# Retention's third outer product of each batch moved a chunk later, its key turns moved ahead, and the join to the next stage reordered

## The chip, the cores and the metric

The kernel runs on one core of one Trainium2 chip. The metric is device time in microseconds (us), the median of several executions. One further execution is recorded by the hardware profiler; its span is the time from the first to the last instruction.

## The reference, cut to what matters

The program is a two-layer decoder on x of shape (2, 512, 256). Layer 0 is a Performer attention, a self and cross attention, and a routed expert block. Layer 1 is a retention, two blocks of softmax attention (a1 on x itself, a2 on a memory), and a routed SwiGLU block. The change touches retention and the first steps of a1:

```python
x = x + L1_attn(layernorm(x), W_qkv, W_o, log_gamma)     # retention, 16 heads of 16
    q, k, v = split((x @ W_qkv.T).reshape(B, L, 3, H, dk))
    k = layernorm(k)
    gamma = sigmoid(log_gamma)
    step: S = gamma * S + v_t[:, None] * k_t[None, :];   y_t = S @ q_t
    y @ W_o.T
x = x + L1_xattn(layernorm(x), ...)                      # first of it: a1
    x = ln(xx, ln1_g, ln1_b)
    a1: xn = ln(x, lnx_g, lnx_b);  yn = ln(x, lny_g, lny_b)
        q = xn @ wq;  k = yn @ wk;  v = yn @ wv;  a = softmax(q k^T / sqrt(32)) ...
```

## The kernel before

Tokens lie in 8 chunks of 128 (4 to a batch, SC = 4; NC = 8), features in FC = 2 blocks of 128. Each engine (TensorE, VectorE, ScalarE, GpSimd as POOL, SyncE) runs its own program; all of them walk the same hand-written list of steps and meet by semaphores. PSUM has 8 banks of 128 x 512 f32, handed out by rings (`Banks.open`): a step that opens a bank waits until its last user has been read out.

Retention is computed in chunks. For chunk c of batch b:
- "scores" (`tensor_scores`, L3632): keys by queries within the chunk, 16 small products into banks 0 to 3, as 32 instructions. VectorE then multiplies them with the decay table (`vector_decay`, L3824, two instructions of 1024 elements), which frees the banks for the next chunk's scores.
- "outer" (`tensor_outer`, L3617): weighted keys by values of chunk i, for i = 0, 1, 2 of each batch. It opens a bank of `ring` (banks 6 and 7). VectorE masks it (`vector_state`, L3806) and adds the decayed earlier state (L3814). The state after chunk i is read by the values of chunk i + 1.
- "key_turn" (`tensor_key_turn`, L3608): the normalised keys (`vector_key_norm`, L3790) turned by TensorE, copied by ScalarE (L3720). Those of batch 1 use `ring` as well, and are needed from the scores of chunk 4 on.
- "values" (`tensor_values`, L3647 for the state's part, L3650 for the chunk's own) into `value_banks` (4 and 5), copied by ScalarE (L3723).
- "rows" (`tensor_rows`, L3661): the output projection of the chunk into `ring`. VectorE adds it to x (L445) and takes the statistics (L281). After chunks 3 and 7 the norm of four chunks follows: a root on ScalarE, scales on VectorE, the application on ScalarE, VectorE and POOL.

The list of steps in the middle, for c from 0 to 9, is: scores c; at c = 0 the three outer products of batch 0; at c = 1 the key turns of batch 1; at c = 2 the three outer products of batch 1; values c - 1; at c = 9 "turn_ahead"; rows c - 2.

"turn_ahead" is the first half of a1's turn: `Turn.tensor` (L382) turns the normalised rows of chunks 0 to 3, one bank of `ring` for each feature block, with six filling matmuls (L175) into the first bank ahead of it. `Turn.scalar_copies` (L398) makes two forms from each bank: `xnT`, for the queries, and `a1ynT`, for keys and values, in the order xnT, ynT of block 0, then xnT, ynT of block 1. VectorE's part of a1's norm for these chunks is done after the rows of chunks 5 and 6 (`ahead`). Then a1's `lead_in` begins: key and query projections (`HeadProjection`, L1810) by turns, and from the fourth projection on the maxima of scores (L1570 on TensorE, L1729 on VectorE) among them. A key projection waits for `ready_x`, which is the last copy of each bank; that same mark frees the bank.

Of the kernel before, what the change touches and what calls it, by code (L numbers as in the profile page):

```python
# [351 lines left out]
class Turn:  # L352
# [35 lines left out]
    def scalar_copies(self, e, w, n):  # L388
        for f in range(self.width // P):
            if not self.by_scalar(f, n):  # L390
                continue
            w.wait_ge(*self.turned.at(self.name, f, n))
            if self.affine is None:
                e.activation(self.dst[:, f, cols(n)], self.view(f, n), ACT.Copy).then_inc(*self.scalar.mark(self.name, f, n))
                continue
            for i, (dst, gain, shift) in enumerate(self.affine):
                w.wait_ge(*self.k.columns.ready.at())
                e.activation(dst[:, f, cols(n)], self.view(f, n), ACT.Identity, bias=shift[:, f:f + 1], scale=gain[:, f:f + 1]).then_inc(  # L398
                    *self.scalar.mark(self.name, f, n, i) if i < len(self.affine) - 1 else self.scalar.mark(self.name, f, n))

# [2553 lines left out]
class Mha:  # L2954
# [4 lines left out]
    def __init__(self, k, pre, before, ready, cross, gain=None, shift=None, norm=None):  # L2959
# [13 lines left out]
        with ExitStack() as mem:  # L2973
# [15 lines left out]
            with ExitStack() as att:  # L2989
# [13 lines left out]
                with ExitStack() as tmp:  # L3003
# [12 lines left out]
                    if not cross:  # L3016
                        self.keys = HeadProjection(
                            k, pre + "_pk", self.attention, self.w["wk"], self.loads["wk"], FC, lambda f, n: self.ynT[:, f, cols(n)], ready_x, self.kT, self.kr)
                for b in range(B):
# [340 lines left out]
class Retention:  # L3360
# [90 lines left out]

    def order(self):

# [7 lines left out]
        for c in range(NC + 2):  # L3461
            if c < NC:
                yield "scores", c
            if c == 0:
                yield from (("outer", (0, i)) for i in range(SC - 1))
            if c == 1:
                yield from (("key_turn", (m, 1)) for m in range(FC))
            if c == 2:
                yield from (("outer", (1, i)) for i in range(SC - 1))
            if 0 <= c - 1 < NC:  # L3470
                yield "values", c - 1
            if c == NC + 1:
                yield "turn_ahead", 0
            if c >= 2:
                yield "rows", c - 2


# [66 lines left out]
    def tensor_program(self, e, w):  # L3544
        opened = False
        for step, i in self.order():
            if step == "scores" and not opened:
# [55 lines left out]
    def tensor_key_turn(self, e, w, m, b):  # L3603
        k = self.k
        bank = (self.ring if b else k.banks).open(w, ("re_kT", m, b), self.k_copied.at(m, b))
        w.wait_ge(*self.knormed.at(b))
# [642 lines left out]
```

## Time and profile before

| | |
|---|---|
| median of 3 runs | 1537.38 us |
| lowest and highest | 1536.84 and 1538.34 us |
| the profiled execution's own time | 1538.35 us |
| its span | 1536.6 us |
| mean granted TensorE clock | 0.987 |
| TensorE busy | 95% of the span |
| scores of chunk 0 begin | 735.23 us |
| a1's first key projection begins | 781.94 us |

Times in views count from the start of the span. The profiled execution's own time lies 1.75 us above its span and 0.97 us above the median of the others. TensorE is PE, its weight loads are PEld. A matmul in f32 appears as two records, a transpose as one. In a timeline, consecutive instructions of one line are merged: the start of the first, the time to the end of the last, and how many. In a window, the numbers are its length, the busy time and count of PE, PEld, DVE, ACT and POOL, then the granted clock, the DMA engines' share and GB/s.

### The profile page before, as it was taken

How to read it: one execution, taken by the hardware profiler on the slowest of the kernel's cores; microseconds unless marked ns; L12 is line 12 of the kernel's file. 1: busy time of each engine (PE TensorE's matmuls, PEld its weight loads, DVE VectorE, ACT ScalarE, POOL GpSimd, SP SyncE). 2: the span in 40 equal slices, each digit the busy share in tenths (PEclk: the TensorE clock that was granted, in tenths of full speed). 3: DMA queues.
4: the chain of work that ended last, by engine and by line, in shares of the span. 5: the costliest groups of instructions: out<-in, count | busy, mean ns of one | idle time of the engine just before them, and what ended most of it. 6: DMA issues, size and time to landing. Idle time of an engine off the chain costs nothing.

```text
span 1536.6 us, 24700 instructions
## 1 busy us (share of the span) xinstructions
PE 1456.1 (95%) x9894; PEld 818.6 (53%) x9894; DVE 851.8 (55%) x1816; ACT 720.3 (47%) x1079; POOL 586.3 (38%) x653
## 2 busy tenths in 40 slices
PE   8999999999999988899899999998999999997997
PEld 5678873333333256796643333653333333766997
DVE  3256627668999564136753784348777772323221
ACT  4544324675666645233254456433555556332331
POOL 3043306223424333521022565502777777405111
PEclk9999999999999999899999999999999999998999
DMA  6000000000110048673000001403000000653000
GB/s 218 1 1 1 1 11 1 8 8 15 49 36 21 3 145 291 206 237 43 7 21 1 1 1 56 124 0 130 1 1 1 1 1 29 242 190 126 9 12 9
DMA packets 75208, 86.94 MB, mean 57 GB/s; under 512 B 27161, under 2 KB 60917, under 8 KB 73942
## 3 DMA queue, kind: packets, MB, share of 16 engines
q1 hardware_dynamic: 72182, 79.10, 16.3%
q0 software_dynamic: 2912, 6.26, 1.1%
q8 instruction: 78, 1.28, 0.3%
q14 instruction: 36, 0.29, 0.1%
HBM read 64.25 MB, written 21.37 MB: 56 GB/s over the span
## 4 chain that ended last, share of the span: by engine, by line
PE 83%; DVE 9%; ACT 3%; issue 2%; POOL 1%; another core or an unknown queue 1%; DMA 0%; POOLq 0%; DVEq 0%; ACTq 0%
PE psum L1606 13%; PE psum L1625 9%; PE psum L1570 7%; PE psum L3997 5%; PE psum L717 4%; PE psum L3263 4%; PE psum L3254 4%; DVE a_nm L1729 3%; PE psum L1810 3%; PE psum L1647 3%; PE psum L4008 2%; PE psum L2740 2%; PE psum L757 2%; PE psum L3232 2%; PE psum L705 2%
## 5 line engine op out<-in xcount | busy, mean ns | idle before, releaser
L1729 DVE TENSOR_REDUCE a_nm<-psum 128x1 f32<-128x512 f32 x384 | 248.9, 685 | 99.5 <-PE psum L1570 87.9
L1729 DVE TENSOR_REDUCE xa_nm<-psum 128x1 f32<-128x512 f32 x256 | 161.7, 682 | 49.5 <-PE psum L1570 44.2
L1660 ACT ACTIVATE a_w<-psum 128x1024 f32<-128x1024 f32 x86 | 83.3, 1021 | 60.7 <-PE psum L1606 60.7
L1660 ACT ACTIVATE xn<-psum 128x1024 f32<-128x1024 f32 (+1 forms) x96 | 86.2, 949 | 51.5 <-PE psum L1606 51.5
L1606 PE MATMUL psum<-a2qT,a2kT 32*128 32x512 f32 x512 | 90.2, 592 | 0.0
L1660 ACT ACTIVATE xa_w<-psum 128x1024 f32<-128x1024 f32 (+2 forms) x96 | 79.7, 886 | 19.2 <-PE psum L1606 19.1
L1570 PE MATMUL psum<-a2kr,a2qr 32*128 32x512 bf16 x256 | 78.1, 384 | 7.4 <-DVE a_nm L1729 5.5
L1570 PEld LDWEIGHTS psum<-a2kr,a2qr 32*128 32x128 bf16 x256 | 20.5, 91 | 108.5 <-DVE a_nm L1729 92.5
L1570 PE MATMUL psum<-xa_ckr,xa_cqr 32*128 32x512 bf16 x256 | 65.7, 382 | 1.7 <-POOL xa_ckr L1857 1.0
L1602 PE MATMUL psum<-a_mrow,onesb 3*128 3x512 bf16 x384 | 62.4, 386 | 3.6 <-DVE a_mrow L1752 1.5
L4064 DVE TENSOR_TENSOR sw_hT<-sw_gt,psum 128x512 f32<-128x512 f32 x22 | 15.0, 688 | 71.3 <-PE psum L3997 43.6
L651 POOL TENSOR_SCALAR pf_kdd<-pf_kdd 128x1024 f32<-128x1024 f32 x8 | 22.2, 2773 | 84.2 <-ACT pf_kdd L830 84.1
L3936 POOL DMA_INDIRECT out<-sw_o,sw_back x11 | 15.2, 1381 | 101.4 <-DVE sw_o L4082 84.2
L1726 DVE TENSOR_REDUCE xa_parts<-psum 128x4 f32<-128x512 f32 x80 | 50.1, 677 | 6.7 <-PE psum L1568 4.4
L1606 PE MATMUL psum<-xa_cq,ctxT 32*128 32x512 f32 x256 | 53.3, 636 | 0.1
L1570 PEld LDWEIGHTS psum<-xa_ckr,xa_cqr 32*128 32x128 bf16 x256 | 17.3, 91 | 65.3 <-DVE xa_nm L1729 47.9
L1660 ACT ACTIVATE ctxT<-psum 128x1024 f32<-128x1024 f32 x40 | 38.8, 1021 | 25.7 <-PE psum L1606 25.0
L1660 ACT ACTIVATE xnT<-psum 128x1024 f32<-128x1024 f32 x40 | 38.8, 1021 | 24.1 <-PE psum L1606 24.1
L1570 PE MATMUL psum<-a1kr,a1qr 32*128 32x512 bf16 x128 | 42.5, 383 | 5.0 <-DVE a_nm L1729 4.0
L1606 PE MATMUL psum<-xa_cq,co_ctx 32*128 32x512 f32 x256 | 46.6, 629 | 0.0
L3997 PE MATMUL psum<-sw_xgT,sw_own 128*128 128x128 f32 x384 | 44.1, 275 | 0.5 <-ACT sw_xgT L4046 0.5
L1606 PE MATMUL psum<-a1qT,a1kT 32*128 32x512 f32 x256 | 44.5, 587 | 0.0
(582 smaller groups left out, 3404.5 us busy)
## 6 DMA issues: line engine op xcount, KB each, us to landing
mo_w<-in_L_ffn_W SPq DMA_DIRECT2D x14, 1024.0 KB
sw_wv<-in_L_ffn_w_v SPq DMA_DIRECT2D x4, 2048.0 KB, 18.7
scratch_a2v<-co_stages SPq DMA_DIRECT2D x16, 256.0 KB
scratch_a2k<-co_stages SPq DMA_DIRECT2D x16, 256.0 KB
a2kT<-scratch_a2k SPq DMA_DIRECT2D x8, 512.0 KB, 8.6
a2v<-scratch_a2v SPq DMA_DIRECT2D x4, 1024.0 KB, 11.6
sw_wp<-in_L_ffn_w_proj SPq DMA_DIRECT2D x4, 1024.0 KB, 19.6
scratch_yd<-zero SPq DMA_DIRECT2D x8, 256.0 KB, 2.2
```

What stands on the lines that cost most here:

```text
L717: t = e.matmul(k.ps[:, bank, :], wt[:, f, chunk(pair)], k.xnT[:, f, cols(n)], start=f == 0, stop=f == FC - 1)
L1570: t = e.matmul(out, query[:, chunk(i)], key[:, part * S:(part + 1) * S], start=True, stop=True)
L1602: e.matmul(ps[:, pr + h % 2, lo:S], self.k.const.onesb[rows, :], self.mrow[n % 3][rows, lo:S], start=True, stop=False)
L1606: t = e.matmul(ps[:, pr + h % 2, lo:S], job.key(h)[:, chunk(c)], job.query(h)[:, lo:S], start=self.folded, stop=True)
L1625: t = e.matmul(ps[32 * h:32 * h + 32, 6, lo:hi], job.value(c, h), self.weights(n, c)[:, h, lo:hi], start=start, stop=last and not upper)
L1647: t = e.matmul(ps[32 * h:32 * h + 32, 7, :], self.k.const.ones[:, 0:32], self.weights(n, c)[:, h, :], start=(n, c) == self.dens(n)[0], sto ...
L1660: e.activation(self.weights(n, c)[:, 2 * jj:2 * jj + 2, lo:S], ps[:, pr:pr + 2, lo:S], ACT.Exp, scale=self.scale).then_inc(*self.weighed.m ...
L1726: e.tensor_reduce(self.parts[n % 3][:, q, part, :], view.rearrange("p (h n) -> p h n", n=P), AX.X, ALU.max, negate=True).then_inc(*self.ma ...
L1729: e.tensor_reduce(self.nm[n % 3][:, q, part, h:h + 1], view, AX.X, ALU.max, negate=True).then_inc(*self.max_taken.mark(*i))
L3254: t = e.matmul(k.ps[:, bank, :], self.li2[:, f, chunk(m)], k.xnT[:, f, cols(n)], start=f == 0, stop=f == FC - 1)
L3263: t = e.matmul(self.k.ps[:, self.k.banks.of(self.rows.name, c), 0:D], self.hT[:, m, chunk(c)], self.li3[:, m, :], start=m == 0, stop=m == ...
L3997: t = e.matmul(k.ps[:, bank, chunk(j)], self.own[i % 2][f][:, features], self.xgT[i % 2][:, chunk(f)], start=f == 0, stop=f == FC - 1)
```

## The change

The list of steps gets a form for TensorE alone, and four things move. The third outer product of each batch comes one chunk later on all engines (at c = 1 and c = 3). The key turns of batch 1 come at c = 0, behind the first two outer products, and use the banks of the values. On TensorE "turn_ahead" comes behind the rows of chunk 7; on the other engines the place stays. And ScalarE makes the keys' form (ynT) of both blocks first and then the queries' form; the key projections of a1 wait for the keys' form alone, while a bank is still free only after its queries' form.

```diff
+            else:
+                self.scalar_affine(e, w, f, n, len(self.affine) - 1)
+        for i in reversed(range(len(self.affine or ()) - 1)):
+            for f in range(self.width // P):
+                self.scalar_affine(e, w, f, n, i)
+
+    def scalar_affine(self, e, w, f, n, i):
+        dst, gain, shift = self.affine[i]
+        w.wait_ge(*self.k.columns.ready.at())
+        e.activation(dst[:, f, cols(n)], self.view(f, n), ACT.Identity, bias=shift[:, f:f + 1], scale=gain[:, f:f + 1]).then_inc(
+            *self.scalar.mark(self.name, f, n, i) if i else self.scalar.mark(self.name, f, n))
+
+    def form_copied(self, f, n, i):
+        return self.scalar.at(self.name, f, n, i)
...
                         self.keys = HeadProjection(
-                            k, pre + "_pk", self.attention, self.w["wk"], self.loads["wk"], FC, lambda f, n: self.ynT[:, f, cols(n)], ready_x, self.kT, self.kr)
+                            k, pre + "_pk", self.attention, self.w["wk"], self.loads["wk"], FC, lambda f, n: self.ynT[:, f, cols(n)],
+                            lambda n: [self.xturn.form_copied(f, n, 1) for f in range(FC)], self.kT, self.kr)
...
-    def order(self):
+    def order(self, tensor=False):
...
             if c < NC:
                 yield "scores", c
+            if c in (0, 2):
+                yield from (("outer", (c // 2, i)) for i in range(2))
             if c == 0:
-                yield from (("outer", (0, i)) for i in range(SC - 1))
-            if c == 1:
                 yield from (("key_turn", (m, 1)) for m in range(FC))
-            if c == 2:
-                yield from (("outer", (1, i)) for i in range(SC - 1))
+            if c in (1, 3):
+                yield "outer", (c // 2, 2)
             if 0 <= c - 1 < NC:
                 yield "values", c - 1
-            if c == NC + 1:
+            if c == NC + 1 and not tensor:
                 yield "turn_ahead", 0
             if c >= 2:
                 yield "rows", c - 2
+        if tensor:
+            yield "turn_ahead", 0
...
-        for step, i in self.order():
+        for step, i in self.order(tensor=True):
...
-        bank = (self.ring if b else k.banks).open(w, ("re_kT", m, b), self.k_copied.at(m, b))
+        bank = (self.value_banks if b else k.banks).open(w, ("re_kT", m, b), self.k_copied.at(m, b))
```

## Rows read from the trace of the kernel before

**Rows 1.** The page: busy time by engine, and the chain by engine

```profile
PE 1456.1 (95%) x9894; PEld 818.6 (53%) x9894; DVE 851.8 (55%) x1816; ACT 720.3 (47%) x1079; POOL 586.3 (38%) x653
...
PE 83%; DVE 9%; ACT 3%; issue 2%; POOL 1%; another core or an unknown queue 1%; DMA 0%; POOLq 0%; DVEq 0%; ACTq 0%
```

**Rows 2.** The chain that ended last, in order of time (start, us, what)

```profile
737.02 2.35 DVE re_w L3824 x2
739.37 0.41 DVE re_state L3806 x2
```

**Rows 3.** Timeline of TensorE, retention (start us, us, engine, line)

```profile
732.90 1.04 PE L3608 MATMUL psum<-ident,re_kt 128*128 128x128 f32 x8
735.23 1.17 PE L3632 MATMUL psum<-re_q,re_kT 32*128 32x128 f32 x32 [1.29 <-ACT re_kT L3720]
736.33 1.16 PE L3617 MATMUL psum<-re_v,re_kw 128*128 128x128 f32 x8
739.82 1.03 PE L3617 MATMUL psum<-re_v,re_kw 128*128 128x128 f32 x4 [2.33 <-DVE re_state L3806]
...
754.07 0.49 PE L3647 MATMUL psum<-re_qg,re_state 128*128 128x128 f32 x2
...
756.06 1.13 PE L3661 MATMUL psum<-rew_woT,re_yT 128*128 128x256 f32 x4
757.12 1.17 PE L3632 MATMUL psum<-re_q,re_kT 32*128 32x128 f32 x32
```

**Rows 4.** Timeline of VectorE, retention

```profile
735.88 1.22 DVE L3790 TENSOR_TENSOR re_kt<-re_kt,re_kst 128x1024 f32<-128x1024 f32 x1
...
740.88 0.49 DVE L3806 TENSOR_TENSOR re_state<-psum,block 128x128 f32<-128x128 f32 x2
741.48 0.61 DVE L3814 SCALAR_TENSOR_TENSOR re_state<-re_state,rew_whole 128x128 f32<-128x128 f32 x2
742.94 2.36 DVE L3824 TENSOR_TENSOR re_w<-psum,rew_decay 128x1024 f32<-128x1024 f32 x2 [0.85 <-PE psum L3632]
```

**Rows 5.** Busy time in chosen windows; the third number from the end is the clock

```profile
739.80:743.40 3.60, 3.58 (x39) 3.13 (x40) 2.54 (x9) 0.00 (x0) 0.00 (x0) 0.54 0.00 0
...
747.70:749.40 1.70, 0.00 (x1) 0.00 (x0) 1.70 (x5) 0.00 (x0) 0.00 (x0) 1.00 0.00 0
749.40:757.10 7.70, 7.62 (x116) 5.48 (x116) 5.24 (x13) 0.77 (x2) 0.00 (x0) 1.00 0.00 0
...
777.60:780.40 2.80, 1.52 (x8) 0.87 (x8) 0.51 (x2) 2.38 (x5) 0.00 (x0) 1.00 0.00 0
780.90:784.40 3.50, 3.50 (x7) 1.63 (x6) 1.79 (x10) 1.22 (x4) 0.00 (x0) 0.52 0.00 0
...
1024.00:1026.00 2.00, 0.81 (x8) 0.60 (x7) 0.80 (x2) 1.45 (x2) 0.00 (x0) 1.00 0.00 0
1026.00:1028.00 2.00, 1.86 (x4) 0.55 (x4) 0.00 (x0) 0.10 (x1) 0.00 (x0) 1.00 0.00 0
```

**Rows 6.** Timeline of TensorE at the join to a1

```profile
776.10 1.46 PE L175 MATMUL psum<-mask_four,identb 128*128 128x512 bf16 x6
777.84 1.57 PE L382 MATMUL psum<-ident,ctxT 128*128 128x128 f32 x8 [0.28 <-DVE ctxT L313]
780.51 1.62 PE L3661 MATMUL psum<-rew_woT,re_yT 128*128 128x256 f32 x4 [1.10 <-ACT a1ynT L398]
781.94 3.19 PE L1810 MATMUL psum<-a1ynT,a1wk 128*128 128x512 f32 x4
784.97 1.88 PE L1810 MATMUL psum<-xnT,a1wq 128*128 128x512 f32 x4
```

**Rows 7.** Timeline of ScalarE at the join: first and last of four copies

```profile
779.01 0.78 ACT L398 ACTIVATE xnT<-psum,cols 128x512 f32<-128x512 f32 x1 [0.42 <-PE psum L382]
...
781.02 0.78 ACT L398 ACTIVATE a1ynT<-psum,cols 128x512 f32<-128x512 f32 x1
```

**Rows 8.** Timeline of VectorE: last of a1's second half norm

```profile
790.13 0.73 DVE L313 TENSOR_SCALAR ctxT<-xn,a_norm_agg,a_norm_std 128x256 f32<-128x256 f32 x2
```

More of the change, by code:

```diff
@@ L394, in scalar_copies @@
                 e.activation(self.dst[:, f, cols(n)], self.view(f, n), ACT.Copy).then_inc(*self.scalar.mark(self.name, f, n))
[L395 to L399, printed above, removed]
+            else:
[10 more added lines that the diff above has]
+        return self.scalar.at(self.name, f, n, i)
     def vector_copies(self, e, w, n):
```

## The prediction

> **What bounds the kernel now.** I read the page first. TensorE is busy 95% of the span and carries 83% of the chain that ended last; VectorE has 9% of it [rows 1]. So time is saved only where the chain leaves TensorE, or where TensorE runs at its lower clock. I then read the chain in order of time over retention. For the first scores it stands on VectorE: the decay product of chunk 0, then the mask of the first outer product, and only then a TensorE instruction [rows 2]. The timeline of TensorE shows the stalls: 2.33 us before the third outer product of batch 0 (739.82) [rows 3], and nothing at all on TensorE from 747.7 to 749.4, ahead of the third of batch 1 [rows 5]. The reason is in the ring of two banks: the third outer product takes the bank of the first, which VectorE masks only after a decay product that lasts 2.35 us. After the first stall the clock was granted at 0.54 over 739.8 to 743.4, and at 1.00 after the second [rows 5]. The third place is the join to a1: row block 7 waits 1.10 us on ScalarE's copies of a1's turn, whose bank it needs, and from 780.9 to 784.4 the clock is 0.52 [rows 5, 6].
>
> **The third outer product a chunk later, the key turns ahead.** Nothing is added or removed: the same matmuls, masks and copies, in another order. I place them one after another.
> TensorE: scores 0 from 735.23 to 736.33 (1.10) and two outer products (1.16 for eight records at full clock) to 737.49 [rows 3]. The two key turns of batch 1 now follow; the keys are normalised at 737.10 [rows 4], just in time, and their banks are those of the values, unused so far. They take 1.04 [rows 3], to 738.53. Scores 1 need both decay products of chunk 0, which end at 739.37 [rows 2]. With 0.14 of lag (my allowance for one wait between engines) they start at 739.51: a wait of 1.0 in place of 2.33, with the turns done.
> They end at 740.61. VectorE masks and carries two outer products, as now, to 740.88, where the third one's mask stands today [rows 4]. That mask and its carry take 1.21 (740.88 to 742.09) and move behind decay 1. So decay 1 starts at 740.9 instead of 742.94 [rows 4], ends at 743.26, and the moved pair ends at 744.4. Meanwhile TensorE does the moved outer product (0.58) and values 0, whose length is below the 1.99 of a full values step (754.07 to 756.06) [rows 3], so it is free at 743.2 at the latest.
> Scores 2 start at 743.40 and end at 744.50; outer products to 745.66 (the second one's bank is masked by 743.8); values 1 (1.99) to 747.65; row block 0 (756.06 to 757.12, 1.06) to 748.71. Decay 2 runs on VectorE from 744.5 to 746.9 and is over when scores 3 start at 748.71: the second stall is gone, covered by values 1 and row block 0. Scores 3 to 749.81, outer product to 750.39 (its bank masked by 748.4), values 2 to 752.38, row block 1 to 753.44. Scores 4 start there; now they start at 757.12 [rows 3]. That is **3.7 us**. From there the order is the old one. The copies of the key turns on ScalarE come earlier, in front of nothing; the values behind them wait for nothing new. SP and POOL are passed by no step: POOL's weighted keys are made before, and SP's next loads wait for the last rows, which come earlier.
> Bounds: the stalls cannot give more than they hold, 2.33 + 1.7 less the new 1.0 and about 0.2 at scores 2, plus the slow stretch, which holds 3.6 us at 0.54 and so hides at most about 1.8: 4.6. From below, if the clock falls again, scores 1 take some 2.2, decay 1 begins at 741.7 and all behind it 0.8 later: 2.9. I take 3.7, since it is made of rows at full clock.
>
> **The last row block ahead of a1's turn.** In times of before, so as to leave the 3.7 out. Row block 7 now needs bank 7 from row block 5 and its copied values, both there; it follows row block 6 at once, 776.2 to 777.3. The six fills (1.46 now, 1.29 back to back) end at 778.55; the turn's first bank is that of row block 6, which VectorE adds while TensorE does row block 7. The first transpose then starts at 778.55 where it starts at 777.84 now [rows 6]; but the last of the first four waits for its chunk now, until about 778.6 (ScalarE starts at 779.01, some 0.4 behind it [rows 7]), so the first bank is full only 0.3 later. The turn ends at 779.6. The second bank needs VectorE's addition of row block 7, which stands behind VectorE's share of a1's norm; the turn needs that share from 777.84 on anyway, and both should be done by 778.6, 0.4 before the bank is asked for. ScalarE copies from 779.3 instead of 779.01 [rows 7].
>
> **The keys' form first.** Four copies of 0.67 pitch (779.01 to 781.02 is three) [rows 7]. Now the first key projection waits for all four and for row block 7, and starts at 781.94 [rows 6]. After the change it waits for two: 779.3 + 0.67 + 0.78 is 780.75, so 780.8. That is **1.15**. The query projection behind it comes at 782.5 and needs all four copies, done at 782.1: covered by the first key projection, with 0.4 to spare; without that cover it would cost up to 1.3.
> The clock is the other half. The first projection lasts 3.19 us, the next, the same four matmuls at full clock, 1.88 [rows 6]: **1.3** lost. TensorE after the change works without a gap from the rows to 779.6 and then waits 1.2. The nearest row is the same join of a2's turn: it was granted 1.00 over 1024 to 1026 with TensorE busy 0.81 of 2.00 us, eight transposes before and one wait in it, and kept it [rows 5]. I take the 1.3 as won; both ends, 0 and 1.3, stay in the range.
> The second half of a1's normalisation hangs on row block 7 and on ScalarE, which takes up the root after the four copies, at 782.1. It now ends at 790.86 on VectorE [rows 8]; if it came no earlier, the first maxima, 2.4 us earlier on TensorE, would wait behind it with two banks to run ahead in: at most about 1 us. Row block 7 is done at 782.1 now and its addition, statistics and scales come before that root; so the root at 782.1 is over 1 us earlier than today's, and I take 0.
> **Sum:** 3.7 + 1.15 + 1.3 = 6.15. The profiled execution took 1538.35, of which 1536.6 is span and 1.75 lies around it; it becomes 1532.2. Against the median of 1537.38, 0.97 lower, the forecast is **1531.2**.
>
> **A rule against it.** The granted clock fell after 777.6 to 780.4, in which TensorE was busy 1.52 of 2.80 with little but transposes, and stayed up after a stretch of 1.7 with nothing in it, at 747.7 [rows 5]. The Trainium skill (TensorE: Matmul & The Clock Gate, Part 4: PE-mode transpose) says that a transpose does not count as busy work for the clock in the way that a matmul does. By that rule the key turns are poor cover at 737.5 and the a1 turn keeps its slow stretch. The rows at 777.6 agree with it, and those at 1024 do not show it. By rule and row together the sum would be 2.9 + 1.15, that is 1533.3; by the rows at 1024, 1531.2.
>
> **The rivals.**
> (a) The clock falls at the key turns, at a1's join, or at both. For it: a fall at each place now, with transposes in one of them. Against: the waits are 1.0 and 1.2 instead of 2.3 and two of about 1.1 around sparse transposes. Price 0.8, 1.3 or 2.1: 1532.0, 1532.5, 1533.3.
> (b) The gain is given back in a1's lead-in: VectorE's and ScalarE's second-half normalisation, or the query projection, becomes late. Price 1 to 2.5: 1532.2 to 1533.7. Against it: both have slack above, though only some tenths for the query.
> (c) The change does not remove retention's waits: the moved masks stand behind decay 1 and 3, and the next outer product finds its bank taken. It is asked for at 745.1 and masked at 743.8, so 1.3 of slack; beyond that every tenth counts. If both waits return in full, only a1's 2.45 stays: 1534.9.
> (d) Slower: the work behind, shifted by 6 us, meets the clock's falls at other stalls. One fall costs 1.3 here (first projection). It takes five to undo the sum, and more than seven for over 0.2% slower; at seven the time is 1540.3, at eight 1541.6. The span has far more waits of 1 to 2 us than falls, so it can be; nothing in the trace points to it. A single one more or less moves the forecast by 1.3 either way.
>
> **How the numbers follow.** The forecast's own case gets 0.60, with 1.3 on each side for one clock fall elsewhere: 1529.9 to 1532.5. (a) gets 0.20, (b) 0.10, (c) 0.07, (d) 0.03. About 0.2%, 3.1 us, is what a measurement of this kernel can tell from no change. The forecast, (a) and (b) lie beyond it: 0.90, less 0.02 for (a) and (b) together: faster 0.88. (c) and that 0.02 are within: 0.09. Slower 0.03. The range reaches from 1529.5 (half of what the bound of 4.6 has over 3.7, and one fall fewer) to 1533.9, which takes in (a) and (b).
>
> **What would show it.** Scores 1 start at 739.5, with the two key turns of batch 1 ahead of them; scores 2 at 743.4; no idle time on TensorE before an outer product; scores 4 at 753.4. Row block 7 directly behind row block 6, then fills, turn, and a wait of 1.2 ended by a copy of a1's ynT; the first key projection at 777.1 (780.8 less 3.7), its four matmuls in 1.7 us at a granted clock of 1.00. The forecast is wrong if the clock is near 0.5 in either place, if an outer product waits on a state, if the first query projection waits on xnT, or if a maximum early in a1 waits on VectorE for over 0.5.

## The result, and the profile after

Twenty executions of each kernel, side by side, gave medians of 1539.88 us before (1536.84 to 1558.49) and 1535.99 us after (1530.66 to 1541.18): the ratio of all executions is 0.9964, with a 95% interval of 0.9947 to 0.9980. The two medians alone give 0.9975, a difference of 3.9 us, and the two means differ by 5.2, since before has one execution at 1558.49. The three runs of before that were shown ahead of the prediction belong to these twenty and are among the faster ones. The forecast of 1531.2 is 0.9960 of their 1537.38. That is inside the interval of the ratio, though not met by the medians; as a time it lies 4.8 us too low and its range, 1529.5 to 1533.9, misses the median.

First the timeline of TensorE after, retention, as in [rows 3]. The line numbers have moved by 12: L3644 is scores, L3629 outer, L3620 key turn, L3662 and L3659 values, L3673 rows.

```profile
734.63 1.17 PE L3644 MATMUL psum<-re_q,re_kT 32*128 32x128 f32 x32 [1.28 <-ACT re_kT L3732]
735.73 1.16 PE L3629 MATMUL psum<-re_v,re_kw 128*128 128x128 f32 x8
736.72 1.04 PE L3620 MATMUL psum<-ident,re_kt 128*128 128x128 f32 x8
738.92 1.17 PE L3644 MATMUL psum<-re_q,re_kT 32*128 32x128 f32 x32 [1.15 <-DVE re_w L3836]
740.02 0.71 PE L3629 MATMUL psum<-re_v,re_kw 128*128 128x128 f32 x4
740.66 1.08 PE L3662 MATMUL psum<-re_w,re_v 128*32 128x128 f32 x32
742.69 1.17 PE L3644 MATMUL psum<-re_q,re_kT 32*128 32x128 f32 x32 [0.95 <-DVE re_w L3836]
...
747.79 1.17 PE L3644 MATMUL psum<-re_q,re_kT 32*128 32x128 f32 x32
748.89 0.71 PE L3629 MATMUL psum<-re_v,re_kw 128*128 128x128 f32 x4
...
752.39 1.17 PE L3644 MATMUL psum<-re_q,re_kT 32*128 32x128 f32 x32
```

The waits in front of an outer product are gone. What is left, 1.15 and 0.95, stands in front of scores and ends with a decay product. From scores 0 to scores 4 it is 752.39 - 734.63 = 17.76 us; before, 757.12 - 735.23 = 21.89.

The same view at the join, as in [rows 6], and ScalarE's copies as in [rows 7]:

```profile
770.40 1.99 PE L3673 MATMUL psum<-rew_woT,re_yT 128*128 128x256 f32 x8
772.23 1.46 PE L175 MATMUL psum<-mask_four,identb 128*128 128x512 bf16 x6
773.53 1.15 PE L382 MATMUL psum<-ident,ctxT 128*128 128x128 f32 x8
775.87 1.96 PE L1819 MATMUL psum<-a1ynT,a1wk 128*128 128x512 f32 x4 [1.19 <-ACT a1ynT L404]
777.66 1.88 PE L1819 MATMUL psum<-xnT,a1wq 128*128 128x512 f32 x4
...
774.28 1.45 ACT L404 ACTIVATE a1ynT<-psum,cols 128x512 f32<-128x512 f32 x2 [0.42 <-PE psum L382]
775.62 1.44 ACT L404 ACTIVATE xnT<-psum,cols 128x512 f32<-128x512 f32 x2
```

Row blocks 6 and 7 are one group, fills and turn follow, and the first key projection starts when the second copy of ynT is done. It lasts 1.96 where it lasted 3.19. From the first scores to the second projection it is 43.03 us, and was 49.74: **6.71 won**. Yet the span fell only from 1536.6 to 1533.9. The windows of after show where the rest went (the clock is the third number from the end):

```profile
734.60:739.00 4.40, 3.22 (x52) 2.92 (x53) 4.27 (x6) 1.15 (x3) 1.50 (x1) 1.00 0.02 6
739.00:743.00 4.00, 3.05 (x77) 2.57 (x81) 3.84 (x9) 0.38 (x1) 0.00 (x0) 1.00 0.00 0
...
775.80:780.00 4.20, 4.13 (x10) 2.01 (x11) 2.70 (x6) 3.75 (x8) 1.58 (x2) 1.00 0.00 0
828.00:832.70 4.70, 3.58 (x27) 1.71 (x27) 2.91 (x5) 3.39 (x4) 0.00 (x0) 1.00 0.00 0
832.70:839.60 6.90, 6.90 (x42) 2.49 (x39) 2.52 (x4) 2.48 (x3) 2.89 (x4) 0.51 0.01 2
...
1051.20:1054.60 3.40, 3.40 (x6) 0.67 (x5) 1.78 (x3) 0.00 (x0) 0.00 (x0) 0.50 1.05 391
1075.10:1078.50 3.40, 3.40 (x22) 1.15 (x22) 2.18 (x4) 0.82 (x1) 1.40 (x2) 0.50 0.00 0
```

The two slow stretches of before, in retention and at the join, are gone. Two new ones have come, in work that the change does not touch: at a1's first scores (832.7 to 839.6) and in a2's lead-in (1051.2 to 1054.6). The one near 1076 was there before as well, and so were those that lie further from the change, between 611 and 638 and near 1406. I measured the program in stretches between the same first instructions in both traces, by their starts:

| stretch | before | after | difference |
|---|---|---|---|
| start to retention's first scores | 735.23 | 734.63 | -0.60 |
| scores 0 to scores 4 | 21.89 | 17.76 | -4.13 |
| scores 4 to scores 7 | 12.08 | 12.08 | 0 |
| scores 7 to a1's first key projection | 12.74 | 11.40 | -1.34 |
| first to second projection | 3.03 | 1.79 | -1.24 |
| to a1's first scores | 52.35 | 52.35 | 0 |
| to a1's first column sums | 12.14 | 14.91 | +2.77 |
| to a2's first query projection | 176.45 | 176.51 | +0.06 |
| to a2's first scores | 47.38 | 48.99 | +1.61 |
| to the end | 463.31 | 463.48 | +0.17 |

The differences sum to -2.70, the change of the span. Nearly all that was given back, 4.38, lies in the two stretches with a new slow clock. So theory T after the result was: the change's own steps won what was forecast, and the remainder is where the clock falls elsewhere. The rival R: a fixed wait of the changed kernel's own takes it back.

### The profile page after: what moved, and what is told of

Read it like the earlier page. It is cut to its first block, busy times and chain, and to the rows that moved or that the text cites. A ratio compares the mean times of both kernels' runs of the same rounds, so it can differ in the third digit from the quotient of the medians.

```text
span 1533.9 us, 24703 instructions
## 1 busy us (share of the span) xinstructions
PE 1455.4 (95%) x9894; PEld 818.0 (53%) x9894; DVE 852.0 (56%) x1816; ACT 720.2 (47%) x1079; POOL 587.2 (38%) x653
## 4 chain that ended last, share of the span: by engine, by line
PE 84%; DVE 9%; ACT 2%; issue 2%; POOL 1%; another core or an unknown queue 1%; DMA 0%; POOLq 0%; DVEq 0%; ACTq 0%
PE psum L1615 13%; PE psum L1634 9%; PE psum L1579 7%; PE psum L4009 5%; PE psum L726 4%; PE psum L3273 4%; PE psum L3264 4%; DVE a_nm L1738 3%; PE psum L1819 3%; PE psum L1656 3%; PE psum L4020 2%; PE psum L2749 2%; PE psum L766 2%; PE psum L3242 2%; PE psum L714 2%
## 5 line engine op out<-in xcount | busy, mean ns | idle before, releaser
L660 POOL TENSOR_SCALAR pf_kdd<-pf_kdd 128x1024 f32<-128x1024 f32 x8 | 22.2, 2774 | 81.4 <-ACT pf_kdd L839 81.3
L2749 PE MATMUL psum<-mo_xgT,mo_w 128*128 128x154 f32 x256 | 37.8, 309 | 7.6 <-DVE mo_xgT L2730 7.4
```

The lines of the kernel that those rows point to most:

```text
L2749: t = e.matmul(ps[:, bank, (m - m0) * 256:(m - m0) * 256 + CAP], w1[:, f, chunk(m)], self.xgT[:, f, x * CAP:(x + 1) * CAP], start=f == 0, ...
```

## The experiments

**Both kernels again, and the two halves of the change.** before_again and after_again are the two files unchanged. ret_only takes back the join, join_only takes back retention's part. The core of each edit against the changed kernel:

```diff
-            if c == NC + 1 and not tensor:
+            if c == NC + 1:
...
-        if tensor:
-            yield "turn_ahead", 0
...
-                            lambda n: [self.xturn.form_copied(f, n, 1) for f in range(FC)], self.kT, self.kr)
+                            ready_x, self.kT, self.kr)
```

for ret_only, with the copies in the old order as well, and for join_only:

```diff
-            if c in (0, 2):
-                yield from (("outer", (c // 2, i)) for i in range(2))
             if c == 0:
+                yield from (("outer", (0, i)) for i in range(SC - 1))
+            if c == 1:
                 yield from (("key_turn", (m, 1)) for m in range(FC))
-            if c in (1, 3):
-                yield "outer", (c // 2, 2)
+            if c == 2:
+                yield from (("outer", (1, i)) for i in range(SC - 1))
...
-        bank = (self.value_banks if b else k.banks).open(w, ("re_kT", m, b), self.k_copied.at(m, b))
+        bank = (self.ring if b else k.banks).open(w, ("re_kT", m, b), self.k_copied.at(m, b))
```

> The kernel before, unchanged, as a control. Theory T (the two profiled executions of before and after agree in their work outside retention and a1's join; what differs there is where TensorE's clock fell): a second profile of the same kernel shows the same 49.7 us from the first scores to a1's second projection, give or take 1.7, but falls of the clock in other places than the first one, and a span that differs from 1536.6 by 1 to 4 us with them. Rival R (the 4 us that after gives back are a fixed wait of its own): the span comes within 0.5 us of 1536.6 and the falls stand where they stood. Ratio to before: 1.000, and the spread of its single times shows what a median of three is worth.

> The changed kernel, unchanged, as a control. T: 43.0 us from the first scores to a1's second projection, as in its first profile; falls of the clock at other places than 832 to 840 and 1051 to 1055, and where one of these is missing, the stretch around it is 1.4 to 3 us shorter than in the first profile of after. R: the stretches from a1's join to the end are again some 4 us longer than in before, wherever the clock falls. Ratio 0.996 to 0.997 for both, as it is the same kernel as the one measured.

> Retention's part alone: third outer products a chunk later and key turns ahead in the values' banks; the join to a1 as before. T: scores 4 begin 17.8 us after scores 0 (before 21.9, after 17.8), and a1's second projection 45.6 after scores 0: before's 49.7 less 4.1, as the join keeps its wait of 1.1 and its slow projection. Ratio about 0.9973. R, in the form that the join eats what retention wins: the join takes more than before's 27.85 from scores 4 to the second projection.

> The join alone: row block 7 ahead of a1's turn and the keys' form copied first; retention as before. T: scores 4 at 21.9 as in before, the second projection 25.3 after scores 4 as in after (before 27.85): 2.6 won, ratio about 0.9983. If the clock falls at the join all the same, 1.3 of it stays away. R: less than 1 us is won, because row block 7 ahead only helps when retention has ended early.

Measured on one chip, twelve executions each, medians: before 1538.08, after 1533.61, retention's part 1535.67, the join's 1540.00. Their ratios to a further 35 executions of before there are 0.9958, 0.9923, 0.9943 and 0.9972. The first of these is the kernel before against itself, and its interval (0.9922 to 0.9994) does not even hold 1: seven of the 35 took 1555 to 1559 us. So medians of a dozen cannot settle parts of 2 us here, and the traces have to.

In the traces the stretches repeat to 0.1 us where the clock is 1.00: scores 0 to 4 took 17.77 with retention's part alone and 17.76 again with all. Join_only took 23.47 where I had expected 21.9, with a slow stretch at each of the old waits, the second of them new. Scores 7 to the first projection took 11.41 with the join's part and 12.74 without. The halves add. Wrong was what I expected of where the clock falls: I had expected other places in a second profile of the same kernel, and from retention on before_again and after_again showed the same stretches slow as their first profiles (a1's first scores to the column sums 12.14 and 14.91). A third profile of each, below, did differ. But ret_only shows none of the new ones: 12.15 there, 47.39 to a2's scores, and a span of 1531.0, which is 2.9 less than the full change, although its join is 1.3 us longer. I had expected a slow first projection there, as in before; it took 1.79 to the second, so 44.4 from the first scores instead of 45.6, although the join's steps are those of before:

```profile
777.64 1.96 PE L1817 MATMUL psum<-a1ynT,a1wk 128*128 128x512 f32 x4 [0.30 <-ACT a1ynT L402]
```

So the slow first projection is no fixed cost of that join. Seven profiles in all have the join of before (before, before_again, before_third, ret_only, outer_only, outer_values and turns_only); in two of them, before and before_again, the projection is slow. R (a fixed wait of the changed kernel) does not fit that, and T (scatter by chance) does not fit the two repeats. Theory T2: a stall late in the program drops the clock or not by the moment at which it comes, so everything that shifts the work moves the falls.

**The same kernel shifted by fills.** Filling matmuls into the bank of a1's first key projection, ahead of its wait:

```diff
-        self.attention.beside.open(w, (self.name, m, n), self.kept_exact(m, n))
+        bank = self.attention.beside.open(w, (self.name, m, n), self.kept_exact(m, n))
+        if self.name == "a1_pk" and (m, n) == (0, 0):
+            self.k.fill(e, w, self.k.ps[:, bank, :], 13)      # 5, 13 or 20
```

hold instead puts fills where the clock fell: four in the wait between the first two score pairs of a1 and a2, and 3, 1, 1 ahead of maxima in a2's lead-in, each in a bank that is opened next anyway.

```diff
+        if self.own_den and (n, c, jj) == (0, self.chunks(0)[1], 0):
+            for point in self.acc_free:
+                w.wait_ge(*point)
+            self.k.fill(e, w, ps[:, 7, :], 4)
...
+                if self.cross and step == "max":
+                    since += 1
+                    if since in (3, 4, 5):
+                        self.fill_beside(e, w, 3 if since == 3 else 1)
```

> The changed kernel with five filling matmuls ahead of a1's first key projection, in the 1.19 us in which TensorE waits there for ScalarE's copies. They delay nothing (five take about 1.1). Theory T2 (which stalls the clock falls at is settled by when the later work arrives, not by this wait): first key projection within 0.2 of 775.9 counted alike from the first scores, and the same slow stretches as the changed kernel, 2.8 lost between a1's first scores and its first column sums and 1.6 before a2's scores. Theory R2 (the clock fell later because TensorE waited at the join): these two are gone, and the span is 4 us shorter, near 1529.5.

> The same with 13 filling matmuls, which delay everything behind by about 1.7 us. T2: the work of a1 arrives about where the retention-only kernel has it (there 96.7 us from the first scores to a1's first scores, 95.4 in the changed kernel), and in the profiled execution the slow stretch at a1's first scores is missing as it is there; the kernel pays 1.7 and gets back up to 2.8 + 1.6: span 1531 to 1533, below the 1533.9 of the changed one though it does more. R3 (the slow stretches belong to the order of the join's steps, whatever the time): both stay, span 1535.6.

> The same with 20, a delay of about 3.2 us. T2 cannot say from one point where the next slow stretches come; if they follow the arrival time alone, they differ from those of the 5 and 13 fills in at least one place. R3: both stay, and the span is 1537.1. Timed runs: each fill beyond five costs 0.216 in every execution, so if falls scatter by themselves, medians rise by 1.7 and 3.2 over the changed kernel, whatever the profile shows.

> The changed kernel with fills at the two places where its clock fell: four in the wait of 0.9 between the first two pairs of scores of a1 (and of a2), and three, one, one in the waits before the third to fifth maxima behind a2's second turn. T2: the slow stretches at 832 and 1051 are gone, and perhaps the one at 1075; 2.8 + 1.6 less about 0.4 for fills that don't fit their waits: span near 1530, ratio against the changed kernel 0.997 to 0.998 in the profiled execution, and a lower median and a narrower spread of the timed ones. If the spread stays as wide, the falls that make it lie elsewhere, before retention too.

| | scores 7 to first projection | a1 scores to sums | a2 projection to scores | span | median |
|---|---|---|---|---|---|
| after (first profile) | 11.40 | 14.91 | 48.99 | 1533.9 | |
| delay5 | 11.40 | 12.15 | 47.39 | 1531.4 | 1536.84 |
| delay13 | 12.85 | 12.15 | 57.36 | 1547.1 | 1539.03 |
| delay20 | 14.36 | 12.14 | 47.38 | 1535.6 | 1540.03 |
| hold (median of five) | 11.41 | 12.14 | 47.84 | 1533.3 | 1535.00 |

On that chip 28 further executions of before had a median of 1541.70.

Five fills delay nothing, and both new slow stretches are gone in the profile. T2 had said that both stay, so by itself this speaks for R2 (the join's wait causes them). But the work before the join came 1.56 us later in that execution (first scores at 736.19, not 734.63), so the moment changed too, and the run tells the two apart less well than I meant it to. Thirteen fills speak against R3 and against R2 for a2's stretch: the order of the steps is the same and the join's wait is filled, a1's stretch is fast, and a2's is 10 us longer. For a1's stretch R2 is weakened only by turns_only below, which has the join of before and is slow there all the same (13.50). The windows of delay13 from a2's turn on:

```profile
1046.00:1053.80 7.80, 6.55 (x32) 3.22 (x30) 5.98 (x14) 4.09 (x8) 4.23 (x4) 1.00 0.69 209
1053.80:1070.00 16.20, 14.63 (x25) 3.33 (x24) 7.87 (x13) 2.26 (x5) 0.00 (x0) 0.50 0.56 207
1070.00:1091.30 21.30, 18.70 (x67) 6.43 (x69) 11.31 (x19) 7.24 (x9) 8.12 (x14) 0.50 0.00 1
1091.30:1100.00 8.70, 8.58 (x72) 2.59 (x65) 6.25 (x11) 5.82 (x6) 7.34 (x6) 1.00 0.00 0
```

One slow stretch, 37.5 us long. So my figure for this run (span 1531 to 1533) was missed by 14, in the direction that T2 leaves open: it says that falls move with the shift, not that they become fewer. Twenty fills gave the same picture as five, one slow stretch at a2's first scores (1076.5 to 1079.9) between the join and 1400, so a shift does not always move a fall. The medians follow the work: 2.2 and 3.2 more than with five fills, for 8 x 0.216 = 1.7 and 15 x 0.216 = 3.2.

T2 is therefore not shown. Each shifted kernel was profiled once, so moment and chance are not parted, and the time from the start of the span does not settle it: a1's first scores began at 831.55 in delay5, which kept the clock, and at 831.96 in after_third, which lost it. What the traces show is that the same stall loses the clock in one execution and keeps it in another.

hold missed as well: a span near 1530 was expected and 1533.3 came. The slow stretches at 832 and 1051 are gone, but a2's first scores have one of 10.2 us, and the four fills there did not stop it, since it begins ahead of them:

```profile
1066.80:1077.00 10.20, 9.87 (x46) 3.39 (x46) 4.91 (x9) 3.82 (x5) 4.96 (x7) 0.50 0.01 2
```

Part of the scatter between executions lies ahead of the change, where the kernels are the same: the first scores began between 733.47 us (before_again) and 741.07 (outer_values), with the clock down for 10.2 and 20.5 us of the time before them.

**One move at a time.** outer_only moves the third outer products and leaves the key turns; turns_only does the reverse; row7_only and form_only split the join.

All four are made from the halves. outer_only, against ret_only:

```diff
-            if c == 0:
+            if c in (1, 3):
+                yield "outer", (c // 2, 2)
+            if c == 1:
                 yield from (("key_turn", (m, 1)) for m in range(FC))
-            if c in (1, 3):
-                yield "outer", (c // 2, 2)
...
-        bank = (self.value_banks if b else k.banks).open(w, ("re_kT", m, b), self.k_copied.at(m, b))
+        bank = (self.ring if b else k.banks).open(w, ("re_kT", m, b), self.k_copied.at(m, b))
```

turns_only, against ret_only:

```diff
-            if c in (1, 3):
+            if c in (0, 2):
                 yield "outer", (c // 2, 2)
```

row7_only, against join_only, with the copies in the old order as well:

```diff
-                            lambda n: [self.xturn.form_copied(f, n, 1) for f in range(FC)], self.kT, self.kr)
+                            ready_x, self.kT, self.kr)
```

form_only, against join_only:

```diff
-            if c == NC + 1 and not tensor:
+            if c == NC + 1:
...
-        if tensor:
-            yield "turn_ahead", 0
```

> Of the four moves only the third outer products, a chunk later; batch 1's key turns stay at c = 1, in the ring's banks; the join as before. By the steps of the prediction the decay product of chunk 0 still ends at the same time and lets scores 1 begin, and TensorE reaches scores 2 with all its work done before decay 1 ends: 17.8 us from scores 0 to scores 4, as with all moves. TensorE then waits 2.0 in one piece ahead of scores 1. If the clock falls in it (rival: the key turns are what keeps it up) it is 18.6.

> Only the key turns ahead, in the values' banks, behind two outer products; the third outer product behind them still at c = 0 and c = 2. The first wait shrinks from 2.3 to 1.2, the second stays (1.8). 20.9 us from scores 0 to scores 4 (21.9 before) if the clock holds at the first wait; rival (the turns count for nothing and the clock falls as before): 21.9 less about 0.3.

> Only row block 7 ahead of a1's turn; copies in the old order, and the key projection waits for all four. From the start of scores 7 to the first key projection: the turn is full 0.3 later and four copies follow, so 12.9 (before 12.74, with both moves 11.40): nothing won. TensorE waits 2.5 there, so the clock most likely falls and the first projection lasts 3.0 as before. Rival (the row block was the bound): 11.4 to 11.7.

> Only the keys' form first; row block 7 still behind the turn, in the bank of the turn's first block, which is free after the queries' form, now the third copy instead of the second: it begins 0.65 later, and the key projection behind it at 13.0 after scores 7 (before 12.74): lost 0.3. Rival (the copies were the bound): 11.6.

This chip is quicker by 22 us for the kernel before too (1515.57 in one execution beside 1510.78, 1513.81, 1518.09 and 1514.30 of these four), so only stretches are compared. turns_only took 20.85 from scores 0 to 4, as expected (20.9): the first wait 1.46 instead of 2.33, the second as before. row7_only took 12.74 from scores 7 to the first projection and form_only 12.94, expected 12.9 and 13.0: each alone wins nothing, together 1.34 (before 12.74, both 11.40). With row block 7 ahead, ScalarE's four copies are the bound; with the keys' form first, row block 7 is, since it waits for xnT. row7_only also has the slow first projection, 3.37.

Three of these kernels also tell what the clock alone was worth in retention, which the first two profiles could not. form_only and row7_only have the steps of before there, with the slow stretch in another place; turns_only has none.

| us from scores to scores | 0 to 2 | 2 to 3 | 3 to 4 |
|---|---|---|---|
| before, slow from 740.1 to 743.5 | 10.21 | 7.53 | 4.15 |
| form_only, slow from 734.9 to 738.3 | 9.17 | 9.02 | 4.15 |
| row7_only, slow from 728.2 to 731.6 | 9.92 | 7.54 | 4.15 |
| turns_only, not slow | 9.17 | 7.53 | 4.15 |

The steps of before at one clock take 9.17 + 7.53 + 4.15 = 20.85, an estimate from these rows. So of the 4.13 won in retention 3.09 is the new order and 1.04 is the slow stretch of before. turns_only takes the same 20.85: the key turns ahead win no time by themselves.

outer_only was the miss: 21.14 where I expected 17.8 (before 21.89). Its timeline of TensorE:

```profile
721.52 1.17 PE L3640 MATMUL psum<-re_q,re_kT 32*128 32x128 f32 x32 [1.29 <-ACT re_kT L3728]
722.62 1.16 PE L3625 MATMUL psum<-re_v,re_kw 128*128 128x128 f32 x8
725.81 1.17 PE L3640 MATMUL psum<-re_q,re_kT 32*128 32x128 f32 x32 [2.03 <-DVE re_w L3832]
726.91 0.71 PE L3625 MATMUL psum<-re_v,re_kw 128*128 128x128 f32 x4
727.46 0.60 PE L3616 MATMUL psum<-ident,re_kt 128*128 128x128 f32 x4
729.88 0.66 PE L3616 MATMUL psum<-ident,re_kt 128*128 128x128 f32 x4 [1.82 <-DVE re_state L3814]
730.47 1.20 PE L3658 MATMUL psum<-re_w,re_v 128*32 128x128 f32 x32
731.59 2.09 PE L3640 MATMUL psum<-re_q,re_kT 32*128 32x128 f32 x32
```

The second key turn waits 1.82 us for a state's mask: in the ring of two its bank is that of the outer product just moved, whose mask stands behind decay 1. It is rival (c)'s mechanism, in a step that the change had moved out of its way.

**Side by side once more, the bank alone, and more fills.** before_third and after_third are the unchanged files. outer_values is outer_only with the key turns in the values' banks. Its edit against outer_only:

```diff
-        bank = (self.ring if b else k.banks).open(w, ("re_kT", m, b), self.k_copied.at(m, b))
+        bank = (self.value_banks if b else k.banks).open(w, ("re_kT", m, b), self.k_copied.at(m, b))
```

hold2 is hold with a fill ahead of the third maximum in a row, and of each further one in that row, from a2's first stretch of maxima behind its second turn on:

```diff
-                    if since in (3, 4, 5):
-                        self.fill_beside(e, w, 3 if since == 3 else 1)
+                    if 3 <= since < 99:
+                        self.fill_beside(e, w, 3 if turned and since == 3 else 1)
...
+            elif step in ("feature", "query", "row"):
+                turned, since = False, 0 if self.cross and since < 99 else 99
```

> The kernel before once more, beside the changed one and on the same chip as it. Its timed executions scatter by several us, with a lower mean clock in the longer ones. Theory T2: the ratio of this kernel to itself is 1.000 within its interval, and medians of changed and unchanged kernel on one chip differ by what the profiles show as fixed, 5.5 us (4.1 in retention and 1.3 at the join, clock aside), give or take the falls of the clock: 4 to 7.

> The changed kernel beside it. T2: 17.76 us from scores 0 to scores 4 and 11.40 from scores 7 to the first key projection, as each time; median 4 to 7 us under the other's, ratio 0.9955 to 0.9975. Rival R (the shift gives the gain back by itself): a difference under 3.

> The changed kernel with fills in the waits of a1's first scores, and in those of a2's lead-in and first scores wherever TensorE waits there for VectorE (third of three maxima in a row, and the tail). T2: no slow stretch between 825 and 1080 in the profiled execution, none of the executions over 1545, and a median 1 to 3 us under the changed kernel's. Rival: the fills cost what they save, because VectorE's maxima are the bound there; then the stretch from a2's first query projections to its first scores is longer than 47.4 at a clock of 1.00.

> The third outer products a chunk later, the key turns of batch 1 at c = 1 as in before, but in the values' banks. It tells whether the move of the outer products alone won little (21.1 us from scores 0 to scores 4 instead of the 17.8 expected) because of the bank or because of the place. If the bank: 17.8 to 18.7, and no wait of a key turn on a state's mask. If the place: 21.1 again.

| twelve executions (hold2 eleven) | median | lowest | highest |
|---|---|---|---|
| before_third | 1544.92 | 1539.96 | 1562.14 |
| after_third | 1536.93 | 1532.66 | 1539.77 |
| hold2 | 1534.37 | 1530.43 | 1536.28 |

Against 28 further executions of before on that chip (1543.69): 1.0014 for the kernel itself (0.9982 to 1.0047), 0.9951 for the changed one (0.9928 to 0.9975; 0.9955 to 0.9975 was expected), 0.9923 for hold2 (0.9892 to 0.9955). The profile of after_third has the 17.76 and 11.40 expected, and its slow stretches beyond the join are where they were, but the one at a1's first scores is shorter (13.50 instead of 14.91). The 8.0 us between the first two rows is above the 4 to 7 expected. The profile of before_third shows other falls than the two before it: retention took 23.24, with two slow stretches, the first projection of a1 was not slow (1.79 to the second), and the clock was down from 1075 to 1089, at a2's first scores. So the same file can fall in other places. That a stall taken out is also a place less for the clock to fall, and so explains the 8.0, fits this and is not shown.

outer_values took 19.23 in retention, with the clock down from 746 to 751 and no wait on a mask. So of outer_only's 3.4 us over the full change 1.9 is the bank. The last 1.5 is the clock: outer_values loses 1.47 between scores 1 and 2, where its slow stretch is, and nothing elsewhere. Without it the run would take 17.76, so the third outer products with the bank carry all that the new order wins, and the key turns ahead help only by where the clock falls. In outer_values it fell 1.5 us behind the plain wait of 2.03 ahead of scores 1; in outer_only, which has the same wait, it fell only at 731.3, behind the key turn's wait of 1.82. It fell in none of the nine profiled executions that have the key turns there and a wait of 1.15 (nor in turns_only). The turns shorten the wait and fill it at once, and no run parts the two.

hold2's windows, over the stretches that were slow in after:

```profile
832.50:837.10 4.60, 4.24 (x29) 1.92 (x30) 2.91 (x5) 3.39 (x4) 0.00 (x0) 1.00 0.00 0
837.10:844.00 6.90, 6.90 (x72) 3.26 (x70) 4.41 (x7) 4.30 (x5) 4.23 (x5) 1.00 0.01 2
1046.00:1053.00 7.00, 6.78 (x33) 3.35 (x34) 5.18 (x13) 4.08 (x8) 4.22 (x4) 1.00 0.67 212
1053.00:1070.50 17.50, 16.64 (x52) 4.85 (x55) 14.40 (x25) 5.62 (x9) 3.17 (x7) 1.00 0.54 200
1070.50:1085.00 14.50, 14.38 (x113) 5.11 (x107) 10.15 (x16) 9.11 (x10) 11.40 (x12) 1.00 0.01 1
```

There is no slow stretch between the first retention scores and 1402. The fills cost little: a2's first query projection to its first scores takes 47.52 with them and 47.38 in before, which is 0.14 and just past the rival's mark of 47.4; first scores to column sums takes 14.55, before 15.90 with a slow stretch in it. The timeline of TensorE at a1's first scores shows how a fill sits in a wait (one of the four has no record):

```profile
835.26 0.49 PE L1579 MATMUL psum<-a1kr,a1qr 32*128 32x512 bf16 x2
835.91 0.81 PE L175 MATMUL psum<-mask_four,identb 128*128 128x512 bf16 x3 [0.16 <-issue]
836.66 0.39 PE L1615 MATMUL psum<-a_mrow,onesb 3*128 3x512 bf16 x2
```

hold2's median is 2.6 us under the changed kernel's on the same chip, and its extremes lie 5.9 us apart against 7.1 and 22.2. The intervals of the two ratios overlap, and on another chip the changed kernel without fills had a median of 1533.61, so that it is faster is likely and not shown.

## Why the prediction was right, and where it was wrong

**Retention, 3.7.** Measured 4.13 in the first traces, of which 3.09 is the order and 1.04 the slow stretch of before; the forecast compared its starts at full clock with a start that lies behind that stretch, and so held both. Each start came within 0.5 us of the forecast once counted from the first scores: scores 1 at 4.29 (forecast 4.28), scores 2 at 8.06 (8.17), scores 3 at 13.16 (13.48), scores 4 at 17.76 (18.21). Scores 4 came 0.45 early. I had taken 1.16 for two outer products and 0.58 for one, which are lengths to the end of the last record, where the next step starts 0.99 and 0.55 after them; the two values steps took 1.94 and 1.89 and not 1.99; and scores 2 started 0.11 early, with decay 1. The covers held: no outer product waits on a state, and the second stall is gone behind values 1 and row block 0.

**The join, 1.15 and 1.3.** Measured 1.34 and 1.24. The second number is luck in part: it is the slow first projection, which only two of seven profiles with the old join have. The wait of 1.2 came as forecast (1.19) and ended on a copy of ynT. Each half of it alone wins nothing, which the steps gave in advance for both.

**The transposes' rule.** By the sum that went with it the time would have been 1533.3, with a slow stretch at the key turns or at the join. The rows of after show 1.00 over both, and so did every profiled execution with both moves. The waits were shorter than before as well, so this does not show that transposes hold the clock up; it shows that they were enough here.

**Rivals.** (a) did not happen in a profile of the changed kernel. (b) did not: 52.35 us from the second projection to a1's first scores in both. (c) did not in the change, and did in outer_only, where a wait on a mask took 1.82. (d) happened in small: falls of the clock at other stalls, priced at 1.3 each, gave back 4.38 in the profiled execution, and 2.97 in after_third's (1.36 at a1's scores, 1.61 in a2's lead-in).

**The step that failed** is the last of "how the numbers follow": "the forecast's own case gets 0.60, with 1.3 on each side for one clock fall elsewhere", set against a median of three. The forecast is 4.8 us too low, and two things make that up.

The first is the base, 2.5 us. The three runs of before, within 1.5 us of each other, looked like a kernel that repeats to 0.1%; its twenty had a median of 1539.88. The sum of 6.15 less than that is 1533.7, inside the range.

The second, the other 2.3, is how the sum treats the clock. It took the slow stretches of before as a fixed part of its time, 1.04 in retention (inside the 3.7) and 1.3 at the join (1.24 in the traces), and it put slow stretches elsewhere at nothing, with one fall each way as the whole scatter. The runs show that the falls are not fixed. At one clock the change is worth 3.09 + 1.34 = 4.43, and the twenty executions differ by 3.9 in the median and 5.2 in the mean. The first profile of the changed kernel had two new slow stretches, worth 2.77 and 1.61. Its twenty executions reach from 1530.66 to 1541.18 and their mean clock from 0.989 to 0.982, the longer the lower.

The profile of before had the hint. Besides the two slow stretches at the change's own places it has one at 1078, at a2's first scores, where TensorE waits for less than 1 us at a time, and others far from the change, near 614, 631 and 1409. I had read the places where the change acts and not the rest.

What stays open: what decides at which stall the clock falls, and how much of the differences of 3.9, 4.5 and 8.0 us between medians is the change's fixed part (4.43 by the traces) and how much the falls. Only the falls of profiled executions were seen.

## What to carry to other kernels

Work out a reordering start by start from pitches, and check for each moved step whose bank it takes: here row block 7 and the keys' form each won nothing alone, since each left the other as the bound, and the third outer product lost 1.9 of its gain to a bank. In this program a gain of a few us arrived in full at its place, and falls of the clock at later stalls took back up to 4.4 us of it. So compare stretches between the same instructions, not spans; price a slow stretch of the kernel before as one that may not be there next time; and give the forecast the scatter of many runs and not of three. Where TensorE waits for about 1 us at a time, a few fills are worth a try: in hold2 they cost 0.14 in a2's lead-in, and its one profile has no slow stretch there.

## What the runs showed of the hardware that I had not expected

The clock stayed at 0.50 for 37.5 us in delay13 (1053.8 to 1091.3) although TensorE was busy 33.3 of them with a2's projections, maxima and first scores; in delay5 the same steps ran at 1.00 but for 3.4 us (1072.4 to 1075.8). The Trainium skill (TensorE: Matmul & The Clock Gate, Part 1) has the clock come back after a stretch of sustained work. Here 33.3 us of work with short waits in it did not bring it back, where the other slow stretches last 3.4 to 13.7 us, and the measurement decides. Why it stayed down is open. Executions of before at 1555 to 1562 us, with a mean clock of 0.968 to 0.971, may have such a stretch, but none of them was profiled.

Two profiles of one kernel had the same stretches slow from retention on, and a third had others, while timed executions of it differ by 10 us and more. And chips differ: on one of those used, the kernel before took 1515.57 us in an execution. In the four kernels profiled there the first scores began at 721.5 to 722.5 (735.23 in before), and the last stage, from its first projection on, took 131.8 us instead of 143.6. They lack the slow stretch of 10.2 us (1409.1 to 1419.3 in before) that all other traces have in it, of 10.2 to 13.7 us. At half the clock that hides some 5 us at most (an estimate). The rest, some 7 us, is waits of up to 1.1 us between single matmuls, here two lines of before, and on that chip the same matmuls follow each other without a wait:

```profile
1405.59 0.27 PE L3997 MATMUL psum<-sw_xgT,ctxT 128*128 128x128 f32 x1 [1.05 <-issue]
1407.70 0.27 PE L3997 MATMUL psum<-sw_xgT,xnT 128*128 128x128 f32 x1 [1.12 <-issue]
```

What TensorE waits for there the trace does not name.
